# Attention stage: the row maxima of a head taken two per step, from one and a half heads ahead to step 17

## The reference

```
Q1, Q2 = (Q[..., :dh], Q[..., dh:])        # dh = 16
K1, K2 = (K[..., :dh], K[..., dh:])
A1 = where(causal, einsum('bhqd,bhkd->bhqk', Q1, K1) * scaling, -inf)
A2 = where(causal, einsum('bhqd,bhkd->bhqk', Q2, K2) * scaling, -inf)
attn = softmax(A1, -1) - lam * softmax(A2, -1)
O = einsum('bhqk,bhkd->bhqd', attn, V)
```

## Time and profile before

| | us |
|---|---|
| median of 3 runs (lowest, highest) | 4366.25 (4363.6, 4369.36) |
| the profiled execution, its own time | 4362.48 |
| its span, first to last instruction | 4360.6 |
| TensorE busy in the span | 3700.6 (85%) |
| VectorE busy | 2467.0 (57%) |
| ScalarE busy | 1754.4 (40%) |
| GpSimd busy | 1706.6 (39%) |

### The profile page before, as it was taken

How to read it: one execution, slowest core, us unless ns; L and a number is a source line. 1 busy time by engine, 2 the same in 40 slices (tenths; PEclk the granted TensorE clock), 3 DMA queues, 4 the chain that set the end, 5 groups by cost and what they waited for, 6 DMA issues and landing times. The chain is left out here.

```text
span 4360.6 us, 69689 instructions
## 1 busy us (share of the span) xinstructions
PE 3700.6 (85%) x21166; PEld 1647.8 (38%) x21231; DVE 2467.0 (57%) x4628; ACT 1754.4 (40%) x3522; POOL 1706.6 (39%) x1117
## 2 busy tenths in 40 slices
PE   6869999999999999999999996753899678896794
PEld 3322333232323232323233323642455445555462
DVE  4456766575757576767676753767211276666102
ACT  2324665666656566666666663110122141111110
POOL 1313555555555555555555554400344231110203
PEclk9978999999999999999999997855899899996897
DMA  4431111111111111111111103210443200001332
GB/s 156 154 120 33 34 37 33 34 35 35 35 35 35 35 35 35 35 36 34 38 33 38 31 9 96 82 40 0 121 91 76 45 24 4 0 0 39 111 111 87
DMA packets 202326, 224.92 MB, mean 52 GB/s; under 512 B 86673, under 2 KB 162706, under 8 KB 195858
## 3 DMA queue, kind: packets, MB, share of 16 engines
q1 hardware_dynamic: 186642, 195.39, 15.3%
q0 software_dynamic: 15360, 25.44, 3.1%
HBM read 139.12 MB, written 80.87 MB: 50 GB/s over the span
## 5 line engine op out<-in xcount | busy, mean ns | idle before, releaser
L638 POOL TENSOR_TENSOR attention_probs<-attention_probs 128x1024 f32<-128x1024 f32 (+2 forms) x640 | 1228.1, 1921 | 1160.2 <-PE attention_ps_o L791 1160.1
L708 DVE TENSOR_REDUCE attention_chunk_max<-attention_ps_m 128x1 f32<-128x512 f32 (+3 forms) x2560 | 1394.2, 604 | 457.4 <-PE attention_ps_m L823 280.6
L683 ACT ACTIVATE attention_probs<-attention_ps_s 128x512 f32<-128x512 f32 (+3 forms) x2560 | 1199.5, 532 | 826.9 <-PE attention_ps_s L772 459.7
L768 PE MATMUL attention_ps_s<-attention_q_stack,attention_k_stack 99*128 99x512 bf16 (+3 forms) x2560 | 821.6, 354 | 91.1 <-ACT attention_probs L683 70.1
L820 PE MATMUL attention_ps_m<-attention_k_stack,attention_q_stack 96*128 96x512 bf16 (+3 forms) x2560 | 772.5, 357 | 48.7 <-DMA attention_v_head<-v_rows 34.5
L791 PE MATMUL attention_ps_o<-attention_probs,attention_v_head 128*32 128x512 f32 (+3 forms) x5120 | 647.4, 558 | 8.6 <-issue 5.0
L768 PEld LDWEIGHTS attention_ps_s<-attention_q_stack,attention_k_stack 99*128 99x128 bf16 x2560 | 234.0, 98 | 668.4 <-ACT attention_probs L683 466.0
L820 PEld LDWEIGHTS attention_ps_m<-attention_k_stack,attention_q_stack 96*128 96x128 bf16 x2560 | 224.9, 97 | 628.7 <-DVE attention_chunk_max L708 490.2
L809 PE MATMUL attention_ps_l<-attention_probs,consts 128*32 128x512 f32 (+1 forms) x2560 | 352.6, 580 | 9.7 <-POOL attention_probs L638 1.0
L734 DVE TENSOR_TENSOR attention_out_sb<-attention_even_sb,attention_odd_sb 64x512 f32<-64x512 f32 x128 | 115.0, 898 | 296.8 <-ACT attention_even_sb L656 290.9
L823 PE MATMUL attention_ps_m<-mask_q_bf,ident_bf 128*128 128x128 bf16 x1024 | 225.5, 223 | 0.0
(11 more groups left out here) (283 smaller groups left out, 4108.8 us busy)
## 6 DMA issues: line engine op xcount, KB each, us to landing
qk_parts<-project_parts SPq DMA_DIRECT2D x64, 384.0 KB, 3.0
heads_out<-attention_out_sb SPq DMA_DIRECT2D x128, 128.0 KB, 2.3
out_heads<-heads_out SPq DMA_DIRECT2D x8, 2048.0 KB, 8.2
experts_w<-in_f_w SPq DMA_DIRECT2D x16, 1024.0 KB, 8.3
attention_q_stack<-qk_parts SPq DMA_DIRECT2D x32, 384.0 KB
attention_k_stack<-qk_parts SPq DMA_DIRECT2D x32, 384.0 KB
experts_w<-in_e_w SPq DMA_DIRECT2D x24, 512.0 KB, 4.8
v_rows<-project_v SPq DMA_DIRECT2D x8, 1024.0 KB, 4.2
```

Source lines behind the costliest of these rows:

```text
L638: pool.tensor_tensor(probs[:, to, :, lo:], probs[:, to, :, lo:], probs[:, k % RING_P, :, lo:], ALU.add).then_inc(pair_ok, 1)
L683: act.activation(probs[:, k % RING_P, a, left(k):], ps_s[(2 * k + a) % RING_S][:, left(k):], ACT.Exp, scale=float(DH) ** -0.5).then_inc(pr ...
L708: last = dve.tensor_reduce(chunk_max[:, a, jq, c:c + 1], ps_m[m % RING_M][:, 0:width(m)], AX.X, ALU.max)
L768: last = pe.matmul(psum[:, lo:], ks[at][0:WITH_MAX, a, kb * P:(kb + 1) * P], qs[at][0:WITH_MAX, a, tq * GROUP + lo:(tq + 1) * GROUP], star ...
```

## The change

`maxima_at` now gives, for a step of a head, whose maxima are taken and which: in steps 20 to 39 the first 42 of the head two ahead (`later`), in steps 0 to 17 the other 38 of the next head (`after`), spread evenly over the steps; steps 18 and 19 have none, and the transposition stands at step 18. In head 0 all 80 maxima of head 1 stand in steps 0 to 17. TensorE waits for the loads of the head two ahead at step 20 instead of for those of the next head at step 2. SyncE writes the three rows of maxima before the store of turn 3 instead of behind it. Products, reductions, transfers and their sizes stay the same in number and shape.

```diff
--- before.py
+++ after.py
@@ -471,7 +471,8 @@
 QUAD = 4
 
 MAXIMA = [(a, jq, c) for a in range(2) for jq in range(K_TILES) for c in range(jq // GT + 1)]
-FIRST_MAX, LAST_MAX, TURN_MAX = 2, 32, 32
+
+BEGIN_MAX, END_MAX = 20, 18
 
 
 def is_first(head):
@@ -540,15 +541,15 @@
             a, jq, c = MAXIMA[m]
             return min(GROUP, (jq + 1) * P - c * GROUP)
 
-        def maxima_at(k, alone):
-
-            if alone:
-                return range(len(MAXIMA)) if k == 0 else ()
-            if not FIRST_MAX <= k < LAST_MAX:
-                return ()
-            work = [2 * GROUP + left(m) for m in range(FIRST_MAX, LAST_MAX)]
-            before, at = sum(work[:k - FIRST_MAX]), work[k - FIRST_MAX]
-            return range(before * len(MAXIMA) // sum(work), (before + at) * len(MAXIMA) // sum(work))
+        def maxima_at(head, k, after, later):
+
+            early, steps_early = len(MAXIMA) * (N_STEPS - BEGIN_MAX) // (N_STEPS - BEGIN_MAX + END_MAX), N_STEPS - BEGIN_MAX
+            if k >= BEGIN_MAX:
+                n = k - BEGIN_MAX
+                return later, range(n * early // steps_early, (n + 1) * early // steps_early)
+            start = 0 if is_first(head) else early
+            n, rest = min(k, END_MAX), len(MAXIMA) - start
+            return after, range(start + n * rest // END_MAX, start + min(k + 1, END_MAX) * rest // END_MAX)
 
         def ends(k, after):
 
@@ -595,7 +596,7 @@
                         wait_apart(sp, score_ok, head.n * 2 * N_STEPS, core.passed)
                         wait_apart(sp, values_ok, head.n * N_STEPS, core.passed)
                     load(later)
-                for turn in range(Q_TILES):
+                for turn in range(Q_TILES - 1):
                     if head is not None and not (is_first(head.n) and turn == 0):
                         store(head.n, turn)
                 if after is not None:
@@ -603,7 +604,9 @@
                     for part in range(3):
                         sp.dma_start(qs[after.at][STACK + part:STACK + part + 1].rearrange(
                             "p a (j t) -> p (a j) t", t=P), max_parts[:, part]).then_inc(parts_in, 16)
-                else:
+                if head is not None:
+                    store(head.n, Q_TILES - 1)
+                if after is None:
                     store(head.n + 1, 0)
 
             def store(head, turn):
@@ -734,15 +737,18 @@
                 dve.tensor_tensor(out[:, slot], even[:, slot], odd[:, slot], ALU.add).then_inc(out_ok, 1)
 
             def step(at_head, next_head, later):
-                head = None if at_head is None else at_head.n
-                after = None if next_head is None else next_head.n
+                if at_head is None:
+                    maxima(next_head.n, range(len(MAXIMA)))
+                    return
+                head = at_head.n
                 for k in range(N_STEPS):
                     ended = ends(k, 3)
-                    if head is not None and ended and not (ended[1] and is_first(head)):
+                    if ended and not (ended[1] and is_first(head)):
                         add_halves(head - 1 if ended[1] else head, ended[0])
-                    if after is not None:
-                        maxima(after, maxima_at(k, head is None))
-                if head is not None and after is None:
+                    whose, items = maxima_at(head, k, next_head, later)
+                    if whose is not None:
+                        maxima(whose.n, items)
+                if next_head is None:
                     add_halves(head, Q_TILES - 1)
 
             run(dve, step)
@@ -846,16 +852,18 @@
 
                 score(head, at, 1, 1)
                 for k in range(0, N_STEPS, 2):
-                    items = [] if after is None else [*maxima_at(k, False), *maxima_at(k + 1, False)]
-                    if after is not None and k == FIRST_MAX:
-                        pe.wait_ge(loaded[other], (next_head.round + 1) * (LOADS * 16))
+                    whose, first_items = maxima_at(head, k, next_head, later)
+                    items = [] if whose is None else [*first_items, *maxima_at(head, k + 1, next_head, later)[1]]
+                    whose_n, whose_at = (None, None) if whose is None else (whose.n, whose.at)
+                    if whose is not None and (k == BEGIN_MAX or k == 0 and is_first(head)):
+                        pe.wait_ge(loaded[whose_at], (whose.round + 1) * (LOADS * 16))
                     more = k + 2 < N_STEPS
                     if more:
                         score(head, at, k + 2, 0)
                         score(head, at, k + 2, 1)
 
                     third = -(-len(items) // 3)
-                    maxima(after, other, items[:third])
+                    maxima(whose_n, whose_at, items[:third])
                     if more:
                         score(head, at, k + 3, 0)
                     elif after is not None:
@@ -866,15 +874,15 @@
                     if not more and after is not None:
                         score(after, other, 0, 1)
                         score(after, other, 1, 0)
-                    maxima(after, other, items[third:2 * third])
+                    maxima(whose_n, whose_at, items[third:2 * third])
                     if more:
                         score(head, at, k + 3, 1)
-                    maxima(after, other, items[2 * third:])
+                    maxima(whose_n, whose_at, items[2 * third:])
                     if k >= QUAD and k % QUAD == 0:
                         ones(head, k // QUAD - 1)
                     elif k == 0 and not is_first(head):
                         ones(head - 1, QUADS - 1)
-                    if after is not None and k == TURN_MAX:
+                    if after is not None and k == END_MAX:
                         turn_maxima(after)
                 if after is None:
                     ones(head, QUADS - 1)
```

## The result

The changed kernel takes 4436.26 us (median of 4 runs, 4433.20 to 4438.59) beside 4367.01 us of the kernel before (4363.60 to 4369.36): a ratio of 1.0159, 95% interval 1.0141 to 1.0176. It is **69 us slower**; the forecast was 44 us faster, and the measured time lies outside the range.

What follows compares the result with a forecast made beforehand. TensorE was taken to set the pace, with holes at the head's turn and spells at 1.2 GHz. The terms -20 - 28 - 7 + 6 + 5 = -44 us gave about 4322 us, range 4288 to 4352.

Steps and rivals of the forecast that it cites:

- Costing nothing: Priced at zero: the wait for loads at step 20, turn 3's store behind the three rows, the transpose at step 18.
- four rivals: Alternatives: hole keeps the clock down (0.13), more is filled (0.15), maxima only move (0.08), store wait in every head (0.09).
- D: Step 14: VectorE's addition waits for the store in every head, 4453 us, or in half, 4385; chance 0.09.
- (1): Turn and halves, without the clock: turn 4.10 to 4.4 us with five maxima, head 70.3 to 69.6; -20 us.
- (2): Turns where the program goes straight on: the spells of 1.2 GHz vanish, 18 x 1.55 = -28 us.
- rival A: Turn of the head: the remaining hole keeps the clock down, the -28 us falls away, 4350 us; chance 0.13.
- C: Steps 2, 10, 18 and 22: the opened holes take 0.7 us each rather than 0.3, 4368 us; chance 0.08.
- (3): Nine turns where the loop jumps back: waits for the maxima's rows go, branch and one spell stay; -7 us.
- (4): Ends: head 0's first half +12.3 us to 45.3, and +0.6 behind; head 30 -6.8; in all +6 us.
- (5): Step 14: VectorE's addition waits for the store issued behind the loads; bounds 0 and 18 us, +5 taken.

Runs made afterwards that it cites:

- experiment 1: The changed kernel with the remainder of the maxima split written into PSUM instead of SBUF: 4351.0 us, ratio 0.9965 to the kernel before.
- experiment 2: The changed kernel with GpSimd adding only 8 columns for each softmax, the rest left out of the sums: 4339.2 us, ratio 0.9939 to the kernel before.
- experiment 3: The kernel before with GpSimd adding only 8 columns for each softmax, the rest left out of the sums: 4362.3 us, ratio 0.9986.
- experiment 5: The changed kernel with the maxima of the head two ahead beginning at step 24 instead of 20: 4375.2 us, ratio 1.0016 to the kernel before.
- experiment 9: The changed kernel with the split's remainder in PSUM and four output buffers instead of two: 4332.2 us, ratio 0.9933 to the kernel before.
- experiment 6: The changed kernel with maxima from step 34 to the next head's 31, transpose at 32, and the last turn's store issued before the loads: 4323.4 us.
- experiment 7: The changed kernel with maxima from step 34 to the next head's 31, transpose at 32; VectorE adds half the output straight from PSUM: 4472.4 us.
- experiment 11: Late maxima (step 34 to 31), remainder in PSUM, store before loads, half added from PSUM, plus nine heads per loop round instead of three: 4260.5 us.

## Why the prediction was wrong

**The step that failed** stands under "Costing nothing": the transpose at step 18 was costed by whether VectorE comes to it in time, and the split behind it got no term at all, with the argument that VectorE's 48 us in 69.6 leave room. That holds only if the split stays as short as it was, 0.25 and 0.28 us, and those durations belonged to its place between two additions of GpSimd. Moved to step 20 it met one at work: 3.1 us instead of 0.5, TensorE stood still behind it, V(20) to V(22) became 2.26 us longer, and 17 heads got a spell of the low clock. Experiments 1, 2, 3 and 5 agree on it: put an operand into PSUM (-85), take GpSimd's work away (-97 after, -4 before), or put nothing behind the split (-61). None of the four rivals named it. D was right about the direction, and the measured 4436 lies between its 4385 and its 4453, but that is luck: the store wait, which is real, costs 14 to 19 us here and not 68 to 136.

**Point by point**, with the term of the sum against the runs:

- (1) The turn: right in an undisturbed head. 4.39 us (4.4), first half 31.9 (31.8), and where the split isn't held a second half of 33.2 (33.4) and a head of 69.5 (69.6). Part of the agreement is luck: the terms named for the first half give 33.44 - 1.8 + 2 x 0.3 = 32.2, not 31.8.
- (2) The clock: right. Where the program goes straight on, no turn of heads 0 to 29 has a spell. Before, 19 of these 22 turns had one (the forecast counted 18 of 21, since it took the last branch of the loop for a jump). The hole that remains, 1.10 us before the score, does not bring one; rival A falls. Whether its being shorter (1.25 before) or the maxima around it did that, no run separates. C falls as well, though not by much at each place: by the starts the waits behind steps 2, 10 and 22 are 1.0 us each in head 17 of experiment 1, where head 23 before had 0.5, 0.8 and 0.4 (each less a spacing of 0.25). They grew by 0.5, 0.2 and 0.6, in the mean midway between the forecast's 0.3 and C's 0.7. The sum over both halves is the forecast one, and no spell follows them in heads 0 to 29. But the new hole of 2.12 us at step 20 brought spells back.
- (3) The loop turns: the gain of 7 us did not come. The loop jumps back eight times, not nine: one of the nine branches takes 83 ns. The eight heads that end in a jump take 73.3 us in the mean in experiment 1 and 73.9 before, where parts (1) and (3) asked for 1.5 us less: 8 x 0.9 = some 7 us are missing. The filling isn't hidden by the branch. Three of the turn's maxima stand ahead of it in TensorE's queue and two behind: in head 12 the first score product behind the branch starts 4.77 us after V(38), where it was 3.72 before, and such a turn takes 7.5 us in the mean in experiment 1 (8 turns) against 5.6 before. In head 12 after, the stretch V(32) to V(6) takes 29.05 us against 25.70 of head 11, and before it took 28.00 with fewer maxima.
- (4) The ends: head 30 right (-7.5 against -6.8). Head 0 mis-sized: its first half takes 48.07 us, not 45.3, with VectorE busy for 43.15 of it, as counted; the rest is waiting at starts, of which 45.3 left too little. In all +19.5 us after, with a held split and a spell of its own at step 20, and +16.5 in experiment 1, against +12.9.
- (5) The store: mis-sized. Its bounds were 0 and 18 us and +5 was taken; experiment 9 shows 14 to 19, and experiment 6, in the late window, 17, so the upper end. In the changed kernel VectorE waits 18 times for 23.4 us in all (4 times for 5.9 before), and behind the three longest, in heads 8, 18 and 23, stands a spell of the clock, as in the earlier trace rows.

Without the held split the kernel takes 4351.0 us (experiment 1), so the forecast of 4322 was too low even without the missed term: a gain of 16 us was left instead of 44. The store (9 to 14 more than taken), the loop turns (7) and head 0 (4) make up 20 to 25 of these 29 us, and all three erred to the same side. The rest is within what runs scatter: the ten runs of experiment 1 lie between 4338 and 4367, and in its profile what lies ahead of head 0 and from head 31 on takes 7 us more than in the profile before. The held split adds the other 85.

## What to carry to other kernels

Before an elementwise operation of VectorE that has all operands in SBUF is moved, look at what GpSimd does at the place it goes to: the duration in the trace holds for the old place alone, and a wait for GpSimd is written into the duration, not into the idle time. The minimum beside the median or the maximum of a group shows such a wait at once (214 against 1350 ns after; 214 against 354, and 682 against 2170, already before); an operand in PSUM takes it away, and so does an order that leaves nothing behind the operation on VectorE. Where an engine paces the kernel and a second one works just behind it, price each operation of the second by what queues behind it, not by its share of busy time.

## What the runs showed of the hardware

- A VectorE operation with SBUF operands alone that begins while GpSimd adds ends at a fixed time behind GpSimd's instruction, in every case of the changed kernel in which it is lengthened: the cast L727 75 to 81 ns and the subtraction L728 140 to 146 ns (31 heads each), the 64x512 additions 540 to 548 ns (108 times). With one operand in PSUM it isn't held (0.28 us in all 32 heads; 0.67 us for the additions in experiment 7, where their mean in the changed kernel is 1.28).
- TensorE's granted clock fell to 1.2 GHz in 19 of 22 turns that go straight on before, behind a hole of 1.25 us (the turn of the earlier trace rows is one of the three without, at clock 1.00 in the earlier trace rows), and in none of them after, behind one of 1.10 us with maxima around it. Behind a hole of 2.12 us in steps 20 to 22, the same in all of heads 0 to 29, it fell in 17 of the 30.
- The first store issued behind a head's loads holds SyncE for 19 to 21 us in the median of each run (up to 24.7 in experiment 6), whichever store that is. The one issued ahead of the loads takes 0.56 us.
- A jump back to the start of a hardware loop costs 3.7 us here, with the spells of the clock that follow it. The branch stands in TensorE's queue for 3.4 and 3.6 us in experiment 11, but the turn is only 2.3 to 2.6 us longer than the others.
